# A wait for every pair of GpSimd's row transfers, in two stages of a four-layer gated kernel

## The reference, cut to what matters

```
x = x + tanh(g_xattn[0]) * L0_xattn(layernorm(x), ctx)
x = x + tanh(g_ffn[0])   * L0_ffn(layernorm(x))        # 8 experts, top 2, capacity 320
x = x + tanh(g_xattn[1]) * L1_xattn(layernorm(x), ctx) # 16 heads of 64: the wide attention
x = x + tanh(g_ffn[1])   * L1_ffn(layernorm(x))        # 8 experts, top 2
x = x + tanh(g_xattn[2]) * L2_xattn(layernorm(x), ctx) # the third attention
...
final = zeros.at[idx].add(out)   # an expert's result rows go back to their tokens
```

## Time and profile before

| | us |
|---|---|
| median of 3 runs | 1766.37 |
| lowest, highest | 1758.09, 1767.57 |
| the profiled execution, its own time | 1775.01 |
| its span | 1773.3 |
| TensorE busy | 1382.5 (78%) |
| VectorE busy | 1011.9 (57%) |
| ScalarE busy | 690.0 (39%) |
| GpSimd busy | 461.2 (26%) |
| its mean granted TensorE clock | 0.868 |

### The profile page before, as it was taken

How to read it: one execution, slowest core, us unless ns; L and a number is a source line. 1 busy time by engine, 2 the same in 40 slices (tenths; PEclk the granted TensorE clock), 3 DMA queues, 4 the chain that set the end, 5 groups by cost and what they waited for, 6 DMA issues and landing times. The chain is left out here.

```text
span 1773.3 us, 26739 instructions
## 1 busy us (share of the span) xinstructions
PE 1382.5 (78%) x9650; PEld 837.1 (47%) x9650; DVE 1011.9 (57%) x2471; ACT 690.0 (39%) x1868; POOL 461.2 (26%) x577
## 2 busy tenths in 40 slices
PE   3677845858989948675886798989978967887998
PEld 2333423635555625353332456565655543344665
DVE  6554551154556643166454667676675864555886
ACT  3233431246656514242334455555542133333121
POOL 1000042244423342342000385858450001000000
PEclk8577867979999978787898799899898978988999
DMA  2443011150000010211000000000000010000000
GB/s 49 127 124 99 11 43 55 38 108 10 4 1 1 1 59 30 85 56 33 8 2 1 1 1 1 1 1 1 1 1 1 1 23 8 9 2 1 7 6 13
DMA packets 66999, 45.40 MB, mean 26 GB/s; under 512 B 17564, under 2 KB 60261, under 8 KB 66869
## 3 DMA queue, kind: packets, MB, share of 16 engines
q1 hardware_dynamic: 61013, 34.48, 7.3%
q0 software_dynamic: 4096, 8.40, 1.8%
q10 hardware_dynamic: 1760, 0.82, 0.2%
HBM read 24.91 MB, written 13.89 MB: 22 GB/s over the span
## 5 line engine op out<-in xcount | busy, mean ns | idle before, releaser
L3191 ACT ACTIVATE L2a_pr<-psum,L2a_negmax 128x512 f32<-128x512 f32 (+3 forms) x256 | 131.9, 526 | 131.8 <-DVE L2a_negmax L3261 73.3
L550 ACT ACTIVATE L1x_praw<-psum,L1x_negmax 128x154 f32<-128x154 f32 x256 | 96.2, 391 | 78.7 <-DVE L1x_negmax L642 78.5
L3059 PE MATMUL psum<-ident,L2a_pr 128*128 128x128 f32 x640 | 96.6, 301 | 34.1 <-DVE L2a_pT L3281 20.0
L312 POOL TENSOR_TENSOR L1x_pm<-L1x_praw,L1x_total 128x1024 f32<-128x1024 f32 x32 | 60.8, 1899 | 159.4 <-DVE L1x_total L648 102.4
L3059 PEld LDWEIGHTS psum<-ident,L2a_pr 128*128 128x128 f32 x640 | 81.1, 156 | 41.3 <-issue 25.1
L1519 DVE TENSOR_REDUCE L0x_negmax<-psum 128x6 f32<-128x924 f32 (+1 forms) x48 | 47.7, 1011 | 79.3 <-PE psum L1065 76.3
L1519 DVE TENSOR_REDUCE L3x_negmax<-psum 128x6 f32<-128x924 f32 (+1 forms) x48 | 47.8, 1011 | 69.2 <-PE psum L1065 58.1
L1519 DVE TENSOR_REDUCE L2x_negmax<-psum 128x6 f32<-128x924 f32 (+1 forms) x48 | 47.8, 1011 | 60.0 <-PE psum L1065 53.0
L642 DVE TENSOR_REDUCE L1x_negmax<-psum 128x4 f32<-128x616 f32 x64 | 50.8, 795 | 54.4 <-PE psum L364 50.6
L1957 DVE SCALAR_TENSOR_TENSOR L3f_acc<-psum,L3f_comb,L3f_acc 128x128 f32<-128x128 f32 x256 | 72.0, 343 | 8.4 <-PE psum L1861 5.0
L2950 POOL TENSOR_TENSOR L2a_pr<-L2a_pr,L2a_total 128x1024 f32<-128x1024 f32 x32 | 60.7, 1896 | 51.4 <-DVE L2a_total L3289 51.4
(11 more groups left out here) (695 smaller groups left out, 3548.3 us busy)
## 6 DMA issues: line engine op xcount, KB each, us to landing
expert_arena<-in_L_ffn_w SPq DMA_DIRECT2D x16, 256.0 KB, 4.9
group_in<-zero SPq DMA_DIRECT2D x2, 1472.0 KB, 11.2
L1f_xs<-group_in SPq DMA_DIRECT2D x10, 256.0 KB, 4.1
group_out<-L1f_ys SPq DMA_DIRECT2D x10, 256.0 KB, 2.6
L1f_gu<-in_L_ffn_gate_up_w SPq DMA_DIRECT2D x8, 256.0 KB, 3.8
slots_in<-zero SPq DMA_DIRECT2D x1, 1280.0 KB, 9.4
L0f_xs<-slots_in SPq DMA_DIRECT2D x5, 256.0 KB, 4.1
resid<-in_x SPq DMA_DIRECT2D x4, 256.0 KB, 5.9
```

The costliest lines, as they stand in the source:

```text
L312: nc.gpsimd.tensor_tensor(pm[:, n % 2].rearrange("p j t k -> p (j t) k"), praw[:, n % 3, :, :, 0:MAIN].rearrange("p j t k -> p (j t) k"), ...
L550: nc.scalar.activation(praw[:, n % 3, j, t, :], psum[:, 2 * u + j, x * CTX:(x + 1) * CTX], ACT.Exp, bias=negmax[:, n % 2, u, j, x:x + 1], ...
L3059: last = nc.tensor.transpose(psum[:, TURN + n // 4, n % 4 * P:(n % 4 + 1) * P], pr[:, m % RING, n * P:(n + 1) * P], core.ident[:])
L3191: ins = nc.scalar.activation(pr[:, i % RING, SEQ * j + lo:SEQ * j + hi], psum[:, bank + j, lo:hi], ACT.Exp, bias=negmax[:, i % RING, e:e + ...
```

## The change

Three places get a wait or a wider one, all in GpSimd's queue, and nothing else changes. In `fetch` of the wide attention GpSimd waits, ahead of the second, third and fourth pair of a batch, until all earlier transfers of that batch have landed. In the third attention it does the same for batches 2 and 3. In `Grouped.scatter` the condition of the wait becomes `n` in place of `k`, so that group 0 waits too, ahead of each pair but its very first; for group 1 nothing changes.

```diff
@@ wide_attention, fetch
                     for k in range(k0, k1):
                         t, r = k // 2, k % 2
                         n = b * QT + t
+                        if k and r == 0:
+                            pool.wait_ge(back[b], 16 * k)
                         nc.gpsimd.indirect_dma_start(...).then_inc(back[b], 16)
@@ narrow_attention, gpsimd
                         for x in range(2 * QT):
                             t, r = x // 2, x % 2
                             n = b * QT + t
+                            if x and r == 0:
+                                pool.wait_ge(fetched[b], 16 * x)
                             nc.gpsimd.indirect_dma_start(...).then_inc(fetched[b], 16)
@@ Grouped.scatter
             for r in range(2):
-                if k and r == 0:
+                if n and r == 0:
                     pool.wait_ge(self.s["spread"], 16 * 2 * n)
                 pool.indirect_dma_start(...).then_inc(self.s["spread"], 16)
```

## The result

The changed kernel took 1784.34 us in the median of 4 executions (1774.49 to 1789.66), the kernel before beside it 1762.98 (1758.09 to 1767.57, 4 executions): a ratio of 1.0125 with an interval of 1.0095 to 1.0155. By the ratio it is slower by 22 us (the medians lie 21.4 apart). The forecast was 1764.0, worked out from 1766.37, the median of three of these four.

A forecast was written before the change was run, and what follows sets the result against it. TensorE, busy for 78% of the span, was the main load, with GpSimd mattering only where somebody waits for it. Start 0, end -1.0 and third attention -1.4 gave -2.4 us: 1764.0 on the median, range 1756 to 1784.

The forecast's parts named there:

- the lateness: TensorE's results reaching their reader 2.6 to 4.3 us late beside unbroken transfer issues; read as caused by them, not shown.
- Start, 0 forecast: Start of the wide attention: GpSimd takes back what VectorE would gain, 0 us, between -2.4 and +6.9.
- Step 0's multiplication after 390: Sign that the forecast is wrong: the wide attention's first multiplication, at 388.52 before the change, starting after 390.
- End, -1.0 forecast: End of the wide attention: prompt handoff to VectorE, scatter's cover just used up, stage change at 656.7 instead of 657.74.
- Third attention, -1.4 forecast: Third attention: added waits all hidden, scores gain if key copies come promptly; -1.4 us, between 0 and -2.4.
- The 1 us of the sum that was said to stay, for the mask row: Third attention: SyncE must write the mask row before the keys, an estimated 1 us that the gain cannot remove.
- (a): Rival: lateness stays as it is; start +1.0, end +0.8, third attention 0, giving 1768.2 us; chance 0.22.
- (b): Rival: lateness lasts as long as the transfers, so pacing holds TensorE's results longer; 16.9 us more, 1783.3; chance 0.16.
- (c): Rival: weight loads crowd batch 2 at the wide attention's start, +6.9 us instead of 0, 1770.9; chance 0.10.
- (d): Rival: batch 2's pairs not slowed, stage change costs 1.2, third attention gains 0.4 more; -7.5 us, 1758.9; chance 0.10.

## Why the prediction was wrong

**The sum was made on an execution that the timed ones did not resemble.** The prediction noted that the profiled execution stood 8.6 us above the median of the runs shown, and carried the difference over as if it had nothing to do with the change. It had to do with it: the profiled execution has the lateness of chips 8 and 15; that the executions timed for the comparison had none is inferred, from their 1758 to 1768 beside 1754 to 1775 on chips 7 and 4 (45 of the 46 there under 1770); none of them was traced. Every credit of the sum was drawn on that lateness; taken off, only costs remain.

**Start, 0 forecast.** On a prompt chip the two rows give +11.7, the ratio 15 us. Two things were mis-sized. With prompt handoffs the multiplication is due at 41.9 after the first fetch, not at 48.3 (340.25 to 388.52), so the cover that was counted on was 6.4 us shorter: batch 1's later landing, which the forecast offset against the lateness, now costs VectorE 5.8 us by itself. And the waits were taken too short. Those of batch 2, forecast at 3.3 each, were 3.0, 3.2 and 3.3 in the first profiled execution, but 3.3 to 5.6 in the five later traces with these waits and the loads beside them; the last two of batch 1, forecast at 1.8, were 2.3 to 3.6 in all six. On chip 7 this made the zeroing end 53.5 us after the first fetch, where the forecast had 48.7. "Step 0's multiplication after 390" had been named as a sign of failure, and it stood there at 392.27. The Trainium skill, SBUF — State Buffer, section "Who interferes with whom", has it that DMA never contends with a compute engine; by that rule no handoff could depend on the pacing of transfers. On chips 7 and 4 nothing contradicts it. On chips 8 and 15 the 13.21 us of the unpaced and the 8.16 of the paced scatter do, if the rule, which speaks of memory ports, is meant to cover a handoff too.

**End, -1.0 forecast.** The mechanism was right: the last issue was forecast to end at 653.2 and the stage change to come at 656.7; they came at 651.4 and 656.38, with the first scatter 1.9 us sooner than in the earlier trace rows. GpSimd's share of a stage change is dearer than the 3.5 taken from the earlier trace rows: from the end of the last issue to VectorE's first row it is 4.93 or 4.94 us in all ten traces in which the scatter waits (651.44 to 656.38, 643.89 to 648.83). What failed is again the credit: with a prompt line 665 VectorE is done at 641.35 on chip 7 and the stage change stands at 642.54, 29.7 after the first scatter issue; the waits make this 35.3. That is 5.6 us, and 0.36% by the ratio.

**Third attention, -1.4 forecast.** By ratio +0.05% on chip 7 and -0.38% on chip 8. The signs are those of the reasoning (a gain only where copies are late); the size on chip 8, 7 us, is more than its trace can account for, and stays open. The 1 us of the sum that was said to stay, for the mask row, had no row behind it. From the first profiled execution to chip 7's, measured from the stage change, the first key copy comes 4.0 us sooner and the first scores 2.8, so 1.2 stay. The waits here took 1.8 to 4.9 us in the changed kernel's first trace and up to 6.3 on chip 8, where 1.8 had been taken.

**The rivals.** (a) falls: the lateness does go. (b) gave 1783.3, next to the result, but not by its mechanism: VectorE's row comes 0.04 us after TensorE's while the paced scatter has 10 us to go. (c) is right in kind, and too small alone. (d) falls: the pairs of batch 2 are slowed, and the stage change waits for GpSimd. The case that decided wasn't among them: that in the executions timed there is no lateness to remove.

**What stays open.** What makes a chip late or prompt. In all traces each chip is one or the other, and the times of the kernel before agree but for the edges (one of 23 at 1775.41 on chip 4, the lowest on chip 15 at 1773.8). Each chip was used in one set only, so no run here separates the chip from the time at which the set ran. Nor does lateness in the rows add up to the 24 us between the levels: 6.4 at the start, 5.1 at the end, and 4.3 in the steps between (from the first multiplication to the first scatter issue, 234.5 against 230.2), where the clock was granted at 0.98 and not 1.00 (this last part goes with the execution and not with the chip: 233.3 and 234.8 in two traces of chip 7, 230.2 in two of chip 15):

```profile
395.00:620.00 225.00, 203.94 (x1313) 131.24 (x1311) 129.30 (x306) 138.09 (x547) 80.48 (x126) 0.98 0.02 3
```
```profile
395.00:620.00 225.00, 204.74 (x1331) 129.99 (x1331) 132.25 (x305) 140.35 (x553) 88.61 (x135) 1.00 0.02 5
```

These 15.8 are the 15.4 between the two spans (1773.3 and 1757.9), but the medians lie 24 apart. Neither of these two executions has the 8 us of the clock's fall in the third attention, and 15.4 and 8 make 23.4. On chips 7 and 4, 40 of 46 executions of the kernel before are under 1765, on chips 8 and 15, 47 of 55 are over 1780. It would fit if most executions on a late chip had this fall and few on a prompt one; the traces, 3 of 8 from the late chips and 4 of 8 from the prompt ones, all but one of them of edited kernels, don't show it. The same goes for the part of the change's 21 us (11.7 and 5.7 in rows) that no row shows.

## What to carry to other kernels

Where the profiled execution lies off the median of the timed ones, find out what it has that they have not before a credit is drawn on it; the timed median without it is the case to price first. A wait that paces row transfers costs its full landing time as soon as the issuing engine is the one that the others wait for, and it delays whoever reads the rows, so give it to every second pair, not to each: two pairs under way had the cure (0.992 on a late chip, from 5 executions) at no price that could be measured on a prompt one (1.0013, 0.9990 to 1.0037), though its trace there has 2.7 us more at the stage change (32.4 against 29.7). An edit that cures something is to be timed on more than one chip.

## What the runs showed of the hardware

- The same kernel took 1760 us on two chips and 1783 on two others, at nearly the same clock (0.872, and 0.866 to 0.868). On the latter, handoffs from TensorE to VectorE came 2.2 to 4.3 us late while GpSimd issued row transfers without a break; in the rows this accounts for 11.5 of the 24 us.
- Pauses of 1.5 us or more between pairs ended this, whether they came from waits on the transfers or, at the start, from memsets (2.25 us); in one trace from a late chip, a pause after every four transfers was enough.
- A pair of batch 0 landed in 1.7 to 2.0 us of waiting, one of batch 2 beside SyncE's weight loads in up to 5.6; held clear of them, in 2.0 to 2.4.
- The stage change behind the wide attention (VectorE's first row of the next stage) came 4.93 to 4.94 us after the end of GpSimd's last transfer issue in ten traces and 1.19 to 1.20 after VectorE's last row in the eight others, where that was later.
